# A two-layer graph kernel: ScalarE's copies behind mask work, stragglers a block later, a quarter of the counts in layer two

## The reference, cut to what matters

```python
h = jnp.maximum(_layernorm(x), 0.0)
# layer 0: graph attention, then a GRU cell
Wh = h @ W;  src = Wh @ a[:F];  dst = Wh @ a[F:]
e = leaky_relu(src + dst.T, 0.2)
att = softmax(where(adj > 0, e, NEG_INF), axis=1)
h_prime = att @ Wh
gi = h_prime @ w_ih.T + b_ih;  gh = h @ w_hh.T + b_hh
r = sigmoid(i_r + h_r);  z = sigmoid(i_z + h_z);  n = tanh(i_n + r * h_n)
x = x + (1.0 - z) * n + z * h
# layer 1: linear, then a product with adj
h = jnp.maximum(_layernorm(x), 0.0)
x = x + adj @ (h @ W1.T + b1)
```

## Time and profile before

| | |
|---|---|
| median of 3 runs | 1651.32 us |
| profiled execution, its own time | 1652.7 us |
| span of the profiled execution | 1650.8 us |
| TensorE matmul busy | 1543.0 us (93%) |
| VectorE busy | 1173.5 us (71%) |
| ScalarE busy | 1024.3 us (62%) |
| DMA moved | 445.59 MB, mean 270 GB/s |
| chain that ended last | TensorE 90% of the span |
| layer one, first product to last | 71.1 to 1189.8 us |
| layer two | 1189.8 to 1643.6 us |

### The profile page before, as it was taken

How to read it: one execution, slowest core, us unless ns; L and a number is a source line. 1 busy time by engine, 2 the same in 40 slices (tenths; PEclk the granted TensorE clock), 3 DMA queues, 4 the chain that set the end, 5 groups by cost and what they waited for, 6 DMA issues and landing times.

```text
span 1650.8 us, 35034 instructions
## 1 busy us (share of the span) xinstructions
PE 1543.0 (93%) x13260; PEld 1334.4 (81%) x13260; DVE 1173.5 (71%) x2414; ACT 1024.3 (62%) x1681; POOL 45.2 (3%) x59
## 2 busy tenths in 40 slices
PE   5457999999999999999999999999999999999998
PEld 5346888888888888888888888888888888888887
DVE  8797999999999999999999999999542000000000
ACT  5788998899988998889988998889300000000000
POOL 0220000000000000000000000000000000000000
PEclk9778999999999999999999999999999999999999
DMA  8449888888888898988889888888526444444430
GB/s 329 170 152 370 305 326 332 333 329 330 328 328 332 325 334 325 337 327 333 328 322 338 323 328 332 332 335 330 199 112 236 172 172 172 172 172 172 171 121 14
DMA packets 79366, 445.59 MB, mean 270 GB/s; under 512 B 9112, under 2 KB 38370, under 8 KB 58850
## 3 DMA queue, kind: packets, MB, share of 16 engines
q1 hardware_dynamic: 73714, 440.35, 71.8%
q10 hardware_dynamic: 5616, 4.79, 0.8%
HBM read 361.18 MB, written 83.92 MB: 270 GB/s over the span
## 4 chain that ended last, share of the span: by engine, by line
PE 90%; DVE 4%; issue 2%; DMA 2%; ACT 2%; DVEq 0%; ACTq 0%
PE A L857 54%; PE A L941 27%; PE GP L880 3%; PE GP L881 2%; DMA h_columns<-AE 1%; PE GQ L899 1%; DVE AE L624 1%; ACT M L456 1%; PE GP L882 1%; PE GP L879 1%; DVE JK L624 1%; DMA X<-in_adjb_dram 1%; PE TG L888 0%; PE TG L866 0%; DVE Y L588 0%
## 5 line engine op out<-in xcount | busy, mean ns | idle before, releaser
L857 PE MATMUL A<-TB,M 128*128 128x259 f16 x8192 | 942.5, 275 | 78.0 <-DVE M L655 40.8
L857 PEld LDWEIGHTS A<-TB,M 128*128 128x128 fp8e4 x8192 | 796.3, 97 | 213.1 <-issue 86.9
L466 ACT ACTIVATE JK<-X 128x4096 uint8<-128x4096 uint32 x124 | 447.1, 3606 | 1.8 <-DMA X<-in_adjb_dram 1.7
L456 ACT ACTIVATE M<-SB,dsteep 128x256 fp8e4<-128x256 f32 x1040 | 427.8, 498 | 0.0
L588 DVE TENSOR_SCALAR Y<-X 128x4096 fp8e4<-128x4096 f32 x128 | 292.4, 2284 | 7.5 <-DMA X<-in_adjb_dram 7.5
L643 DVE TENSOR_SCALAR M<-SB,nd 128x256 fp8e4<-128x256 f32 x1008 | 283.4, 354 | 4.8 <-issue 4.1
L768 DVE SCALAR_TENSOR_TENSOR hp<-A,R 128x256 f32<-128x256 f32 x32 | 13.6, 424 | 373.1 <-PE A L941 371.4
L941 PE MATMUL A<-WG,X 128*128 128x256 f16 x2048 | 225.5, 273 | 0.9 <-DVE WG L725 0.9
L941 PE MATMUL A<-WG,TB 128*128 128x256 f16 x2048 | 224.9, 273 | 0.0
L941 PEld LDWEIGHTS A<-WG,X 128*128 128x128 fp8e4 x2048 | 200.3, 98 | 24.2 <-DVE WG L725 1.1
L941 PEld LDWEIGHTS A<-WG,TB 128*128 128x128 fp8e4 x2048 | 200.4, 98 | 23.2
(11 more groups left out here) (133 smaller groups left out, 716.4 us busy)
## 6 DMA issues: line engine op xcount, KB each, us to landing
X<-in_adjb_dram SPq DMA_DIRECT2D x128, 2048.0 KB, 8.9
mask_bytes<-Y SPq DMA_DIRECT2D x128, 512.0 KB, 3.6
X<-mask_bytes SPq DMA_DIRECT2D x16, 2048.0 KB, 9.2
TB<-mask_bytes SPq DMA_DIRECT2D x16, 2048.0 KB, 9.1
M<-in_xb_dram SPq DMA_DIRECT2D x8, 512.0 KB, 8.4
h_rows<-M SPq DMA_DIRECT2D x8, 512.0 KB, 7.1
R<-in_xb_dram SPq DMA_DIRECT2D x32, 128.0 KB, 7.9
R<-h_rows SPq DMA_DIRECT2D x32, 128.0 KB, 7.5
```

The costliest lines, as they stand in the source:

```text
L456: ins = nc.scalar.activation(rows(mask1(c), jj), SB[u][:, :], ACT.Sigmoid, scale=STEEP, bias=dsteep[:, j:j + 1], saturate=False)
L466: nc.scalar.activation(to, X[c % 2][:, :].bitcast(u32), ACT.Sign, accum_out=nz[:, bass.ts(g, 1), c:c + 1].rearrange("p g c -> p (g c)")).t ...
L857: ins = nc.tensor.matmul(A[t][m][:, 0:2 * TW + 1], rows((mask1, mask2)[m](c), jj)[:, t * P:(t + 1) * P], TB[:, c * JC + jj, m, 0:2 * TW + ...
```

## The change: what it does

1. `ON_ACT` goes from 8 to 10: in slots 1 to 31 ScalarE makes 10 of 16 masks of a block and VectorE 6.
2. Layer one counts only blocks 0 to 2 of slots 1 to 31 (`EARLY` = 3). The 4 counts of slot 0 and the counts of block 3 of the other 31 slots, `LATE` = 35, are done in layer two: ScalarE's queue loads the 2 MB of adj again, into two buffers Z in the space of the masks M, and ScalarE counts them. SyncE's load of the next X waits for a count only where there is one.
3. On ScalarE, `hpT` moves from behind the masks of block 2 to behind those of block 3; `rz` from the end of block 3 to the next slot's block 0; `nn` from block 0 to block 1; `h2T` and `WG<-GQ` go one slot on, to blocks 0 and 1. Each stands right behind the masks of its block and ahead of its count.
4. On VectorE, `gated`, `updated`, `normed` and `low_part` go one block later. On TensorE, the transposes of `normed` go from behind block 0 to behind block 1, and `projected` from behind block 1 to behind block 2.
5. In layer two the last small steps stand between six spans of 58 matmuls over three row blocks instead of four of 60 over two. The stores of the result go to SyncE's queue. The tally of the counts is a step of its own ahead of block 28, TensorE's matmul that reads it stands behind block 28, and the verdict behind block 29.

```diff
-ON_ACT = 8
+ON_ACT = 10
+EARLY = CS - 1
+LATE = (NS - 1) * (CS - EARLY) + CS
...
# SyncE, slot
-                                sp.wait_ge(c_cnt, g * CS + c + 1)
+                                if c < EARLY and not (isinstance(g, int) and g == 0):
+                                    sp.wait_ge(c_cnt, (g - 1) * EARLY + c + 1)
                                 sp.dma_start(X[b][:, :], adjb[g * CS + c + 2, :, :]).then_inc(c_in[b], 16)
-                        if c == 1 and in_range(g, 2):
+                        if c == 2 and in_range(g, 2):
                             x1_store(g - 2, u)
...
# SyncE, layer two
                         sp.wait_ge(q_o, k * 4 + b - 3)
+                        store(k * 4 + b - 4, b % 2)
                         x1_load(k * 4 + b - 2, b % 2)
...
# ScalarE, slot
                             sign_mask(g, u, k, c)
-                        if c == 0 and in_range(g, 2):
-                            q = g - 2
-                            act.wait_ge(d_tmp, q + 1)
-                            nc.scalar.activation(nn[:, :, :], tmp[:, :, :], ACT.Tanh).then_inc(g_3, 1)
+                        if c == 0:
+                            if in_range(g, 3):
+                                normed_columns(g - 3)
+                            if in_range(g, 2):
+                                gate_sigmoids(g - 2)
+                        if c == 1:
+                            if in_range(g, 3):
+                                projected_high(g - 3)
+                            if in_range(g, 2):
+                                candidate(g - 2)
+                        if c == 3 and in_range(g, 1):
+                            attended_columns(g - 1)
                         if main:
-                            if isinstance(g, int) and g == 0:
-                                count(g, u, k, c)
-                            if c < CS - 1:
-                                if not (isinstance(g, int) and g == 0):
+                            if c + 1 < EARLY:
+                                if not first:
                                     count(g, u, k, c + 1)
-                            elif not (isinstance(g, int) and g == NS - 1):
+                            elif c == CS - 1 and not final:
                                 count(g + 1, 1 - u, k + u, 0)
                         if c == 1 and in_range(g, 1):
                             evacuate(g - 1)
...
# ScalarE, layer two
+                late = [(0, c) for c in range(CS)] + [(g, c) for g in range(1, NS) for c in range(EARLY, CS)]
+                act.wait_ge(c_pe, NS * CS)
+                for n in range(LATE + 2):
+                    if n >= 2:
+                        g, c = late[n - 2]
+                        act.wait_ge(c_in[n % 2], (NS * 2 + n // 2) * 16)
+                        act.wait_ge(c_cnt, (NS - 1) * EARLY + n - 2)
+                        nc.scalar.activation(junk, Z[n % 2].bitcast(u32), ACT.Sign,
+                                             accum_out=nz[:, g:g + 1, c:c + 1].rearrange("p g c -> p (g c)")).then_inc(
+                                                 c_cnt, 1)
+                        act.wait_ge(c_cnt, (NS - 1) * EARLY + n - 1)
+                    if n < LATE:
+                        g, c = late[n]
+                        act.dma_start(Z[n % 2], adjb[g * CS + c, :, :]).then_inc(c_in[n % 2], 16)
...
# VectorE, layer two
+                def tally():
+                    dve.wait_ge(c_cnt, NS * CS)
+                    nc.vector.tensor_reduce(odd[:, :, 0:1], nz[:, :, :], AX.X, ALU.add).then_inc(k_df, 1)
...
+                with dve.Fori(1, NS // 4 - 1) as k:
                     for b in range(4):
                         finish(k * 4 + b, b % 2, b, k * 2 + b // 2)
+                tally()
+                for t in range(NS - 4, NS):
+                    finish(t, t % 2, t % 4, t // 2)
+                    if t == NS - 3:
+                        judge()
...
# TensorE, behind each block
+                def after(g, u, k, c):
+                    if c == 0 and in_range(g, 1):
+                        attended(g - 1)
+                    if c == 1:
+                        if in_range(g, 1):
+                            pe.wait_ge(g_1, g)
+                        if in_range(g, 2):
+                            normed(g - 2)
+                        if in_range(g, 1):
+                            gates(g - 1, 1 - u, k if u else k - 1)
+                    if c == 2 and in_range(g, 2):
+                        projected(g - 2)
...
# TensorE, layer two
+                for t in range(NS - 4, NS):
+                    rest(t, t % 4, t // 4)
+                    if t == NS - 4:
+                        pe.wait_ge(k_df, 3)
```

More of the change, by code:

```diff
@@ L133, in binary_adjacency @@
         junk = JK[:, 0:JC * RW // 4].bitcast(u8)
-        early_junk = R[:, 0:4, :].rearrange("p r k -> p (r k)").bitcast(u8)
+        Mf = M[:, :, :].rearrange("p c k -> p (c k)").bitcast(f32)
+        Z = [Mf[:, b * JC * RW:(b + 1) * JC * RW] for b in range(2)]
         stx = JK[:, 0:NT * 6].rearrange("p (t k) -> p t k", k=6)
@@ L209, in each_row_block @@
         def each_row_block(eng, slot, last=0):
-            for g in range(2):
-                slot(g, g, 0)
-            with eng.Fori(1, NS // 2 - last) as k:
+            for g in range(4):
+                slot(g, g % 2, g // 2)
+            with eng.Fori(2, NS // 2 - last) as k:
                 for u in range(2):
@@ L502, in slot @@
                             evacuate(g - 1)
[L503 to L509, removed]
@@ L520, in _ @@
                 each_row_block(act, slot, 1)
-                for g in range(NS, NS + 2):
+                for g in range(NS, NS + 3):
                     slot(g, g % 2, g // 2)
-                def store(t, u):
-                    act.wait_ge(q_o, t + 1)
-                    act.dma_start(out[:, bass.ts(t, 2), :], HS[u].rearrange("p (t f) -> p t f", f=F)).then_inc(
-                        q_out[u], 16)
-                with act.Fori(0, NS // 2) as k:
-                    for u in range(2):
-                        store(k * 2 + u, u)
@@ L744, in slot @@
                         if c == 0 and in_range(g, 2):
-                            updated(g - 2, u, k - 1)
+                            gated(g - 2)
                         if c == 1:
                             if in_range(g, 2):
-                                normed(g - 2, u)
+                                updated(g - 2, u, k - 1)
                             if in_range(g, 1):
                                 attended(g - 1)
-                        if c == 3:
+                        if c == 2:
                             if in_range(g, 2):
-                                low_part(g - 2)
-                            if in_range(g, 1):
-                                gated(g - 1)
+                                normed(g - 2, u)
+                            if in_range(g, 3):
+                                low_part(g - 3)
                 each_row_block(dve, slot, 1)
-                for g in range(NS, NS + 2):
+                for g in range(NS, NS + 3):
                     slot(g, g % 2, g // 2)
@@ L863, in attended @@
                 def attended(q):
+                    wait(pe, g_4, q - 1)
                     pe.wait_ge(d_hp, q + 1)
@@ L931, in slot @@
                                 ins.then_inc(e_t0, 1)
-                        if c == 0:
-                            transposes(g)
-                        if c == 1:
-                            linears(g, u, k)
+                        after(g, u, k, c)
                 each_row_block(pe, slot)
@@ L945, in span @@
                     return ins
-                early, nearly = NT - 4, NT - 2
-                pe.wait_ge(d_lo, NS - 2)
+                early = NT - 6
+                pe.wait_ge(d_lo, NS - 3)
                 pe.wait_ge(q_in[0], 16)
@@ L951, in _ @@
                 span(0, 0, 0, 0, early)
-                transposes(NS)
+                after(NS, 0, NS // 2, 0)
                 span(0, 0, 1, 0, early)
-                linears(NS, 0, NS // 2)
+                after(NS, 0, NS // 2, 1)
                 pe.wait_ge(q_in[1], 16)
-                for d in range(2):
-                    span(1, 1, d, 0, early)
-                transposes(NS + 1)
-                pe.wait_ge(d_lo, NS - 1)
-                for b in range(2):
-                    for d in range(2):
-                        span(b, b, d, early, nearly)
-                linears(NS + 1, 1, NS // 2)
-                pe.wait_ge(d_lo, NS)
-                for b in range(2):
-                    for d in range(2):
-                        ins = span(b, b, d, nearly, NT)
+                span(1, 1, 0, 0, early)
+                after(NS, 0, NS // 2, 2)
+                span(1, 1, 1, 0, early)
+                after(NS + 1, 1, NS // 2, 1)
+                pe.wait_ge(e_ev[1], NS)
+                pe.wait_ge(q_in[2], 16)
+                span(2, 2, 0, 0, early)
```

(6 more changed lines are left out.)

89 lines of the change are left out of this document (45 added, 44 removed).

## The result

The changed kernel takes 1625.26 us, the median of 4 runs, against 1651.17 before. The ratio is 0.9844, with an interval of 0.9813 to 0.9875: 21 to 31 us faster, 26 by the middle. The four runs lie at 1617.35, 1620.33, 1630.20 and 1636.04 us; the kernel before spreads over 1.1 us. So there are two things to explain, a gain of up to 34 us and a spread of 19 us that was not there.

A forecast was written before the change was run, and what follows sets the result against it. It took a ring of TensorE and ScalarE, 33.76 us a slot, to bound the kernel. Terms 31.4 + 3.9 + 1.1 = 36.4 us took the profiled 1652.7 to 1616.3, less 1.4 for the median: 1615, range 1609 to 1630.

The forecast's parts named there:

- The ring of a slot: Layer one, TensorE and ScalarE waiting on each other: gaps of 0.83 us and 30 restarts of 0.16 go, 31.4 us.
- The end of slot 0: ScalarE at slot 0's end: `evacuate` begins at 136.2 instead of 140.17, gaining 3.9 us.
- The start of layer two: TensorE entering layer two: one wait of 0.9 us on `low_part` and its restart go, 1.1 us.
- The late counts: Layer two: 35 counts at 9.5 us each end 40 us ahead of need, so they cost nothing.
- A: Layer one: DMA becomes the bound; 1628 us at 335 GB/s, 1646 at 329; chance 0.10.
- B: Layer two: late counts overrun if DMA holds 360 GB/s; TensorE stands 22 us behind block 28, 1637 us; chance 0.04.
- C: Layer two: late loads don't overlap, 13.4 us a count, TensorE stands 96 us behind block 28, 1711 us; chance 0.04.
- D: Layer one: TensorE waits for another moved step in all slots, so no change, 1648 to 1651 us; chance 0.04.
- the three signs of being wrong: TensorE idle over 10 us in layer one after slot 1; X loads over 12 us; last late count in last 60 us.

The follow-up runs named there:

- the second profiled execution: Profiled execution of the changed kernel run again with no edit: 1635.97 us; the runs' median was 1634.83 us.
- The repeated kernel: The changed kernel run again with no edit: 1634.83 us, ratio 0.9866, runs from 1619.84 to 1636.98.
- The best version: Against the changed kernel: nine masks on ScalarE, all counts of slots 1 to 31 in layer one, only slot 0's four counts late; 1615.48 us.

## Why the prediction was right in layer one and wrong in layer two

*The ring of a slot, 31.4 us.* Right. The slot is 32.76 us where 32.77 was worked out, and ScalarE is 2.1 us early where 2.0 was. The gaps are gone, also as to their cause: with nine masks in the old order they grow as the ring says (1675 expected, 1676.43 measured), and with the new order and eight masks they go. Ten masks and three counts aren't needed for it: nine masks and all counts of slots 1 to 31 give the same slots.

*The end of slot 0, 3.9 us.* Right in sum. Slot 1 begins at 136.52 instead of 140.90, 4.4 us; 0.4 of that was there before slot 0. Undone, it costs 3.9.

*The start of layer two, 1.1 us.* Right as a step: no wait for `low_part` is left.

These three make 1614.9; the kernels without most of the 35 loads measure 1615.39 and 1615.48.

*The late counts, 0 us.* This is the step that failed: "So they cost nothing", and in it the sentence that mask loads "may take twice that and still land within the 42 us of three blocks". The question that I worked out, whether 35 counts end in time, has the answer that I gave it, with more room: 8.6 us each, not 9.5, 77 us ahead, not 40. But that they were faster is the other side of what failed. I took 394 GB/s for the sum; the engines gave 428, and the late loads took what they could of it. The mask loads, on a queue that also holds two small transfers a block, landed in 25.7 us at the median and 37.1 at most, and they were not issued 42 us ahead either: in the second profiled execution the mask load issued at 1238.02 followed a store that had waited for `finish` until 1236.59, and `finish` had waited for an x load behind the masks. The masks cost TensorE 3.3 us of waits in one execution and 17.0 in another. The price of the step, measured as the difference to the kernel without loads, is 10 us by the first median (1625.26 - 1615.39) and 19 by the second (1634.83).

What the runs show of the cause: the loads (without them nothing spreads), and the share of SyncE's queue (with masks alone on it they land in 13.4 to 14.0 us at the same total). It is not the order in which that queue is filled, since it never ran empty, nor the delay of the load of block 5 behind `examine`. The share is lost to the small transfers: beside the late loads a packet of 1 KB costs SyncE's queue as much as the late loads' queue spends on one of 16 KB, 145 packets against 145 in 6 us. The prediction priced the traffic by bytes, of which the small transfers are a ninth of SyncE's 2.36 MB a block; by packets they are two thirds, 256 of 384. Why one execution falls into the step of two late loads a block and another doesn't is open.

*Rivals.* A (DMA bounds layer one) is out: 340 GB/s at a share of 0.92, and TensorE never waits. B had the right resource and the wrong place: the sum of rates had no ceiling at 360, the late counts never overran, and TensorE waited for masks instead. The Trainium skill (DMA: Bandwidth & Descriptors, Specifications) gives about 358 GB/s as the limit of HBM for one core; this core, running alone, moved 428 GB/s over 170 us, nearly all of it reads, so the measurement decides against it here. The same section's 435 GB/s as the ceiling of the fabric agrees with the 428 at a share of 1.01. C and D did not occur. Nor did any of the three signs of being wrong: TensorE had no idle time in layer one after slot 1, X loads took at most 10.7 us, and the last late count ended 128 us before the end of the span. None of them looked at the landing of mask loads.

That the measured time lies in the range is luck. The forecast's own range ended at 1625, on the measured median, by bounds of parts that all came out as worked out; the rest of the range was there for half of rival A, which did not occur. The repeated kernel's median, 1634.83, lies outside it. A range for a resource taken to its limit should have held the spread of 19 us.

## What to carry to other kernels

When three engines are all near 95% and one chain goes through two of them, look for the ring before shares: here the reordering gave 24 us in the slots with the masks divided as before, 31 with one mask moved as well, and moving the same mask in the old order cost 24. Background work on a second DMA queue is not free because it ends in time; ask what the foreground's loads take to land while it runs, count the foreground's packets and not only its bytes, keep small transfers off its queue, or pace the background by the engine that is to be spared (1616.5 instead of 1625 to 1635 us). The best version (1615.48) was the one that needed almost no background work.

## What the runs showed of the hardware

- The DMA engines gave 428 GB/s for 170 us, mostly reads in packets of 16 KB from two queues, at a share of 1.01.
- With two queues at this limit, 2 MB loads on the one (35 of them, nothing else on it) landed in 13.6 us, and 2 MB loads on the other, which also held two transfers of 128 KB a block, in 25.7. With the small ones on a third queue: 13.1 and 13.4 to 14.0.
- With small transfers at the head of one queue and 2 MB loads in the other, the queues sent packets one for one: 163 (0.15 MB) against 162 (2.38 MB) in 6 us. Alone, the same small packets went at 252 in a microsecond instead of 27.
- The same small transfers had packets of 1 KB from SyncE's queue and of 4 KB from GpSimd's.
- The changed kernel has two patterns under this load, one with no waits and blocks of 13.97 us, one with waits in each block and 15.3 us, and stays in either for a hundred us and more.
- ScalarE's read of an accumulator (0.19 us) overlaps the next instruction, so that a count of 3.6 us costs 3.6 back to back.
- With nine masks and the new order, VectorE and ScalarE at 96 to 97% busy did not make TensorE wait once in 870 us; in the order before, with VectorE at 97% and ScalarE at 90%, it waited in every slot.
